# Normalisation on GpSimd, context copy on VectorE, one logits matmul per four heads, value product in four column groups, eight weight stage slots

## The reference

```python
def attention_layer(x, Wq, Wk, Wv, Wf, bf, mask):        # layers 0 and 2, 6 heads of 64
    q, k, v = heads(x @ Wq + bq), heads(x @ Wk + bk), heads(x @ Wv + bv)
    scores = einsum('bhqd,bhkd->bhqk', q, k) / sqrt(64)
    probs = softmax(scores + where(mask, 0.0, NEG))
    return merge(einsum('bhqk,bhkd->bhqd', probs, v)) @ Wf + bf

def graph_layer(x, adj, W, b, w_src, w_dst, H_w, H_b):   # layers 1 and 3, 12 heads of 32
    h = einsum('bnd,ade->bane', x, W)
    src, dst = tanh(h) @ w_src, tanh(h) @ w_dst
    a = leaky_relu(src + swap(dst), 0.2)
    a = softmax(where(adj, a, -999.0))
    f = elu(merge(a @ h) + b)
    g = sigmoid(x @ H_w.T + H_b)
    return g * f + (1 - g) * x
```

## Time and profile before

| | |
|---|---|
| median of 3 runs | 2199.91 us |
| profiled execution | 2200.55 us |
| its span, first to last instruction | 2198.6 us |
| busy: TensorE matmul / weight load | 2068.9 us (94%) / 1909.4 us (87%) |
| busy: ScalarE | 2061.2 us (94%) |
| busy: VectorE / GpSimd | 1626.4 us (74%) / 1501.2 us (68%) |
| mean granted TensorE clock | 0.98 |
| chain that ended last | PE 76%, ACT 15%, DVE 4%, POOL 2% |

### The profile page before, as it was taken

How to read it: one execution, slowest core, us unless ns; L and a number is a source line. 1 busy time by engine, 2 the same in 40 slices (tenths; PEclk the granted TensorE clock), 3 DMA queues, 4 the chain that set the end, 5 groups by cost and what they waited for, 6 DMA issues and landing times.

```text
span 2198.6 us, 57665 instructions
## 1 busy us (share of the span) xinstructions
PE 2068.9 (94%) x19852; PEld 1909.4 (87%) x19852; DVE 1626.4 (74%) x3887; ACT 2061.2 (94%) x7066; POOL 1501.2 (68%) x2698
## 2 busy tenths in 40 slices
PE   1699999999999999999769999999999999999994
PEld 1599999999999999999669999999999999999983
DVE  2377878777787878787657787878787877878774
ACT  1499999999999999999869999999999999999996
POOL 0167777777777777777546777777777777777764
PEclk9799999999999999999979999999999999999998
DMA  3100000010100000010110100000010100000000
GB/s 107 48 21 28 27 26 30 24 32 24 32 23 28 28 28 28 25 42 23 45 49 23 32 24 28 28 28 28 24 31 25 32 24 29 27 28 24 13 16 18
DMA packets 65464, 66.04 MB, mean 30 GB/s; under 512 B 22038, under 2 KB 64924, under 8 KB 65180
## 3 DMA queue, kind: packets, MB, share of 16 engines
q1 hardware_dynamic: 65180, 62.37, 9.3%
HBM read 37.18 MB, written 25.17 MB: 28 GB/s over the span
## 4 chain that ended last, share of the span: by engine, by line
PE 76%; ACT 15%; DVE 4%; POOL 2%; issue 1%; DMA 1%; SPq 1%; POOLq 0%; DVEq 0%; ACTq 0%
PE psum L642 31%; PE psum L652 15%; PE psum L634 6%; ACT LG L401 4%; PE psum L719 4%; PE psum L747 4%; PE psum L758 4%; PE psum L683 3%; ACT LA L395 2%; PE psum L694 2%; PE psum L689 2%; PE psum L703 2%; PE psum L733 1%; ACT LG L454 1%; ACT QKT L409 1%
## 5 line engine op out<-in xcount | busy, mean ns | idle before, releaser
L401 ACT ACTIVATE LG<-LG,neg_max 128x128 f32<-128x128 f32 x1536 | 601.5, 406 | 8.9 <-DVE neg_max L573 8.5
L548 DVE CUSTOM_DVE_ANT_0 LA<-psum,neg_bias 128x128 f32<-128x128 f32 x768 | 172.4, 287 | 341.6 <-PE psum L719 341.6
L376 POOL TENSOR_TENSOR prod<-th,vec 128x384 f32<-128x384 f32 x256 | 255.2, 1019 | 184.8 <-ACT th L460 184.8
L401 ACT ACTIVATION_READ_ACCUMULATOR LG<-LG,neg_max 128x1 f32 x1536 | 314.7, 205 | 0.0
L395 ACT ACTIVATE LA<-LA,neg_max 128x128 f32<-128x128 f32 x768 | 302.6, 437 | 2.4 <-DVE neg_max L548 2.4
L569 DVE COPY_PREDICATED_SCALAR LG<-no_edge,no_edge_score 128x1536 f32 x128 | 244.2, 1908 | 2.3 <-ACT LG L454 2.3
L573 DVE TENSOR_REDUCE neg_max<-LG 128x12 f32<-128x1536 f32 x128 | 224.4, 1753 | 13.6 <-DVE LG L569 0.5
L314 POOL TENSOR_SCALAR var_eps<-mv 128x1 f32<-128x1 f32 x256 | 56.8, 222 | 257.2 <-DVE mv L530 176.4
L652 PE MATMUL psum<-hT_hi,qk_hi 128*128 128x256 f32 x1152 | 208.2, 289 | 3.2 <-DVE hT_lo L516 3.2
L642 PE MATMUL psum<-hg_hi,gT_hi 128*128 128x384 f32 x768 | 203.6, 373 | 0.5 <-DVE gT_lo L553 0.5
L652 PE MATMUL psum<-hT_lo,qk_hi 128*128 128x256 f32 x1152 | 197.7, 281 | 0.0
(11 more groups left out here) (125 smaller groups left out, 6400.5 us busy)
## 6 DMA issues: line engine op xcount, KB each, us to landing
xin<-x SPq DMA_DIRECT2D x64, 192.0 KB, 2.3
x_mid<-x SPq DMA_DIRECT2D x64, 192.0 KB, 1.9
xin<-x_mid SPq DMA_DIRECT2D x64, 192.0 KB, 2.3
out<-x SPq DMA_DIRECT2D x64, 192.0 KB, 1.9
stage<-w_qk SPq DMA_DIRECT2D x8, 288.0 KB, 3.0
stage<-w_vf SPq DMA_DIRECT2D x8, 288.0 KB, 3.0
stage<-w_hg SPq DMA_DIRECT2D x8, 288.0 KB, 2.9
adj<-adj SPq DMA_DIRECT2D x32, 64.0 KB, 2.4
```

The source lines that it names most:

```text
L376: last = pool.tensor_tensor(prod[:, i, :], th[:], vec[:, r.pair(k - 2), 2 + i, :], ALU.mult)
L401: last = act.activation(head, head, ACT.Exp, bias=neg_max[:, 1, a:a + 1], accum_out=den[:, a:a + 1])
L548: last = dve.tensor_tensor_reduce(LA[:, i * N:(i + 1) * N], bank(6 + i // KC)[:, (i % KC) * N:(i % KC + 1) * N], neg_bias[:, (k) % 2, :], ...
```

## The change

- The normalisation of the attention layer's input moves from ScalarE to GpSimd, as one operation with two per-node scalars and without the ReLU; the ReLU is taken by ScalarE's copy of the transposed features and by VectorE's subtraction.
- The graph context is copied out of PSUM by VectorE.
- Logits: two transposes give source and target scores with ones beside them; VectorE multiplies the target rows by a selector into `sdR` (96 rows, 4 x 128 columns), and one matmul of 512 columns per four heads makes the whole sum.
- The value product c takes each head in two halves of 32 columns, so it uses four column groups, and stands directly behind the graph context's product.
- Stage slots: 8 instead of 2. The first pair's weights come in 14 pieces, split in steps -4 to 0. The second pair's weights are split by GpSimd in 14 steps of the first pair, kept in DRAM, and loaded in place after the last use of the old ones.
- Selectors come from the identity matrix instead of by DMA; the gate's bias is split on GpSimd, in two steps of the start.
- The order of each engine's step is new, the steps run from -5 to 133, and s runs two steps further ahead of the graph layer's stages.

```diff
+STAGES = 8
...
-        stage = sb("stage", [128, 2, KC, D // 2])
+        stage = sb("stage", [128, STAGES, KC, D // 2])
+        ahead_hi = sb("ahead_hi", [128, 2, KC, D // 2], F32R)
...
-        sel_stage = x1[0:QUADS * GROUP, 0:2, 0:4]
+        sel_stage = gate[0:ROWS, 0, 0:4]
...
-        CHANGES = {-2: range(0, 4), 0: range(4, 6), 2: range(6, 12)}
+        SPLIT_STEPS = {-4: range(0, 3), -3: range(3, 6), -2: range(6, 8), -1: range(8, 11), 0: range(11, 14)}
...
-        sdT_ps = psum[0:QUADS * GROUP, 3, 512 - N // 2:512].bitcast(BF16)
+        sdT_ps = psum[0:ROWS, 6, 512 - N:512].bitcast(BF16).rearrange("p (i n) -> p i n", i=2)
...
+            def load_piece(m):
+
+                name, region, at, n = PIECES[m % len(PIECES)]
+                if m >= len(PIECES) + STAGES:
+                    j = m - len(PIECES) - STAGES
+                    sp.wait_ge(s[f"ahead_out{j % 2}"], 32 * (j // 2 + 1))
+                elif m >= STAGES:
+                    sp.wait_ge(s["w_split"], m - STAGES + 1)
+                sp.dma_start(stage[:, m % STAGES, :, 0:n], REGIONS[region][0][m // len(PIECES)][:, at:at + n].rearrange("(c p) n -> p c n", p=128)
+                             ).then_inc(w_in[m % STAGES], 16)
+
+            def keep_piece(j):
+
+                name, region, at, n = PIECES[j]
+                sp.wait_ge(s["ahead_lo"], j + 1)
+                sp.dma_start(ahead[region, 0][:, :, at:at + n], ahead_hi[:, j % 2, :, 0:n].bitcast(F32)).then_inc(s[f"ahead_out{j % 2}"], 16)
+                sp.dma_start(ahead[region, 1][:, :, at:at + n], stage[:, (len(PIECES) + j) % STAGES, :, 0:n]).then_inc(s[f"ahead_out{j % 2}"], 16)
+
+            def load_next(name):
+
+                region, at = whole(name)
+                for i in range(2):
+                    sp.wait_ge(s[f"ahead_out{i}"], 16 * len(PIECES))
+                for i in range(2):
+                    sp.dma_start(REGIONS[region][1 + i][:, :, at].bitcast(F32), ahead[region, i][:, :, at]).then_inc(w_next[name], 16)
...
-            sp.wait_ge(s["setup_pool"], 1)
-            for i, src in enumerate((sel_src, sel_dst)):
-                rows = src.rearrange("(p k q a) n -> q (p k) a n", p=PARTS, k=2, q=QUADS)
-                for q in range(QUADS):
-                    for pk in range(2 * PARTS):
-                        at = q * GROUP + 4 * pk
-                        sp.dma_start(sel_stage[at:at + 4, i, :], rows[q, pk][:, 4 * q:4 * q + 4]).then_inc(s["const_in"], 16)
...
+                for p in range(2):
+                    if k == B - 3 + p + -1:
+                        for i in [0, 2, 1]:
+                            sp.wait_ge(s[f"qk_ps{i}"], B - 1 + p)
+                            load_next(f"c{p}{i}")
...
+                if k == B - 4:
+                    sp.wait_ge(s["m_v"], B)
+                    load_next("V")
+                if k == B + 1:
+                    sp.wait_ge(s["g_h_ps"], B)
+                    load_next("h")
+                if k == B - 1:
+                    sp.wait_ge(s["o_ps"], B)
+                    load_next("O")
+                if k == B + 1:
+                    sp.wait_ge(s["g_gate_ps"], B)
+                    load_next("gate")
...
+                    wait_latest(pool, r, ("m_hT", k + 3))
+                    b = (k + 4) % SLOTS
+                    pool.tensor_scalar(hM[:], xin[:, b, :], rstd[:, 0, b:b + 1], shift[:, 0, b:b + 1], ALU.mult, ALU.add).then_inc(s["m_h"], 1)
...
+            def head_bias(pair):
+
+                row = hb_row[:, pair, :]
+                at = 9 * pair
...
+                j, odd = divmod(k - AHEAD_STEP, SPREAD)
+                if odd == 1 and 1 <= j < len(PIECES) + 1:
+
+                    j -= 1
+                    m = len(PIECES) + j
+                    n = PIECES[j][3]
+                    src = stage[:, m % STAGES, :, 0:n]
+                    pool.wait_ge(w_in[m % STAGES], 16 * (m // STAGES + 1))
+                    if j >= 2:
+                        pool.wait_ge(s[f"ahead_out{j % 2}"], 32 * (j // 2))
+                    pool.tensor_copy(ahead_hi[:, j % 2, :, 0:n], src).then_inc(s["ahead_hi"], 1)
+                    pool.wait_ge(s["ahead_hi"], j + 1)
+                    pool.tensor_tensor(src.bitcast(F32R), src, ahead_hi[:, j % 2, :, 0:n].bitcast(F32), ALU.subtract).then_inc(s["ahead_lo"], 1)
+
...
-                    act.activation(gcT[:], bank(7)[:, 0:D], ACT.Copy).then_inc(s["gc"], 1)
-                    normed(0, k + 4, xin[:, (k + 4) % SLOTS, :], hM[:]).then_inc(s["m_h"], 1)
+                    act.activation(hT_hi[:, :, (k + 4) % 4, :], chunks(bank(2)), ACT.Relu).then_inc(s["m_hi"], 1)
...
+                    dve.wait_ge(s["g_sdT"], r.done(k - 4))
+                    dve.tensor_tensor(sdR[:, (k - 4) % 2, :, :], sdT_ps[:, 1, :].unsqueeze(1).broadcast_to([ROWS, 4, N]),
+                                      sel[:].unsqueeze(2).broadcast_to([ROWS, 4, N]), ALU.mult).then_inc(s["g_sdR"], 1)
...
+                    dve.scalar_tensor_tensor(hT_lo[:, :, (k + 3) % 4, :], chunks(bank(2)), 0.0, hT_hi[:, :, (k + 3) % 4, :].bitcast(F32),
+                                             ALU.max, ALU.subtract).then_inc(s["m_lo"], 1)
...
+                    dve.wait_ge(s["gc_ps"], r.done(k - 5))
+                    dve.tensor_copy(gcT[:], bank(7)[:, 0:D]).then_inc(s["gc"], 1)
...
+                    picks = idf[0:ROWS, 0:ROWS].rearrange("p (m a) -> p a m", a=4)
+                    dve.tensor_reduce(sel_stage, picks, AX.X, ALU.add).then_inc(s["sel"], 1)
+                    dve.wait_ge(s["sel"], 1)
+                    dve.tensor_copy(sel[:], sel_stage).then_inc(s["setup_dve"], 1)
...
-                    for q in range(QUADS):
-                        pe.matmul(bank(3 + q).rearrange("p (a n) -> p a n", a=4), sdT[rows[q], (k - 3) % 2, :],
-                                  sel_s[rows[q], :].unsqueeze(2).broadcast_to([GROUP, 4, N]), start=True, stop=False)
-                    for a in range(4):
-                        for q in range(QUADS):
-                            last = pe.matmul(bank(3 + q)[:, a * N:(a + 1) * N], sel_d[rows[q], a:a + 1].broadcast_to([GROUP, 128]),
-                                             sdT[rows[q], (k - 3) % 2, :], start=False, stop=(a == 3))
-                    last.then_inc(s["z_ps"], 1)
...
+                    for q in range(QUADS):
+                        rows = slice(q * GROUP, (q + 1) * GROUP)
+                        last = pe.matmul(bank(4 + q), sdT[rows, (k - 3) % 2, :], sdR[rows, (k - 3) % 2, :, :].rearrange("p a n -> p (a n)"), start=True, stop=True)
...
-                        half = slice(h % 2 * MD, (h % 2 + 1) * MD)
-                        last = pe.matmul(bank(2)[half, h // 2 * N:(h // 2 + 1) * N], v[:, (k - 1) % 4, h * MD:(h + 1) * MD],
-                                         PTA[:, i * N:(i + 1) * N], start=True, stop=True)
...
+                        for e in range(2):
+                            rows = slice(h % 2 * MD + e * GD, h % 2 * MD + (e + 1) * GD)
+                            last = pe.matmul(bank(0)[rows, h // 2 * N:(h // 2 + 1) * N], v[:, (k + 1) % 4, h * MD + e * GD:h * MD + (e + 1) * GD],
+                                             PTA[:, i * N:(i + 1) * N], start=True, stop=True)
...
+                    for i in range(2):
+                        last = pe.transpose(sdT_ps[:, i, :], sd3[:, (k - 2) % 4, i * ROWS:(i + 1) * ROWS], idb[:])
...
+            def weights(name, g):
+
+                if g == 0:
+                    pe.wait_ge(s["w_split"], READY[name])
+                    pe.nop(nofuse=True)
+                elif g == B:
+                    pe.wait_ge(w_next[name], 32)
+                    pe.nop(nofuse=True)
```

More of the change, by code:

```diff
@@ L268, in _ @@
+            for m in range(8, len(PIECES)):
+                load_piece(m)
             for i in range(4, SLOTS):
@@ L387, in _ @@
+            run_steps(step, setup)
         @block.scalar
@@ L772, in step @@
[L772 to L782 removed]
+                    wait_latest(pe, r, ("pt", k + 1), ("m_val", k + 3), ("g_gate", k - 3))
```

688 lines of the change are left out of this document (350 added, 338 removed).

## The result

| | before | after |
|---|---|---|
| time, median of 4 runs each (us) | 2198.84 (2195.94 to 2201.46) | 2124.06 (2123.84 to 2124.53) |
| profiled execution, its span (us) | 2200.55, 2198.6 | 2124.53, 2122.7 |
| one steady step (us) | 15.92 | 15.69 |
| s of graph 0 / graph 6 starts (us) | 72.84 / 167.77 | 45.87 / 116.29 |
| from s of graph 6 to s of graph 124 (us) | 1917.2 | 1876.2 |

The ratio is 0.9661 (95% interval 0.9644 to 0.9677): 3.4% faster, 74.8 us where 113 were forecast.

The account below looks back on a forecast made before the run. TensorE's instructions were taken as the limit, ScalarE 0.1 us behind: start -60, steady steps -38.4, middle -35.6, weight splits +15 and drain +6 make -113 from 2199.9, so 2087 us, range 2048 to 2150.

Parts of the forecast that it names:

- the likeliest case: Whole kernel: TensorE's instructions set the step, total 2087 us (2050 to 2120); chance 57%.
- the second case: Steady step: the chain over GpSimd, or VectorE, sets it at 16.0 us, splits cost 12 more, total 2147; chance 22%.
- TensorE's sum, -0.37: Steady step on TensorE: its instructions fall from 15.92 to 15.55 us (15.45 to 15.70); 15.6 was taken.
- The twelve go: -0.32: Steady step on TensorE: dropping the twelve short logits matmuls saves their 0.32 us.
- -0.15: Steady step on TensorE: a layout turn before the value product and the slow first transpose behind s go, saving 0.15 us.
- +0.10: Steady step on TensorE: the new second transpose of the score parts costs 0.10 us (0.05 to 0.15).
- Splits, +15: 14 steps of the first layer pair: weight pieces split on GpSimd in its chain add 15 us (0 to 27).
- Middle, -35.6: Weights of the second layer pair: the 38.6 us lost there go, with 3 left for a late piece.
- Start, -60: Start: small DMAs and the wait for weights go, GpSimd gets the head bias; gain 60 us (25 to 80).
- Drain, +6: End: two more short steps cost 10 us, a shorter own step saves 4 (0 to +20 together).
- the fourth: Start: it brings only its 25 us, as loads and GpSimd's bias rows queue, total 2122; chance 14%.
- The fifth: Ends and step: the ends gain but the step doesn't, as layout turns eat the twelve matmuls, total 2125; chance 2%.

Follow-up runs that it names:

- Experiment 6: The kernel before without the twelve 128-column logits matmuls of the destination scores, nothing else changed: step 15.87 us, one run of 2191.5 us.
- experiments 7 to 9: The changed kernel with the context copy, the normalisation, or both back on ScalarE: one run each, 2131.1, 2112.5 and 2154.4 us.
- Experiment 5: The changed kernel with one whole-array 512-column logits matmul replacing three on row groups from the 28th step: step 15.41 to 15.47, one run of 2105.6 us.
- experiment 4: The changed kernel with the value product in two column groups of 64 in place of four of 32: step 15.84, one run of 2139.7 us.
- experiment 3: The changed kernel with GpSimd's normalisation issued twice from the 25th step on: step 16.21, one run of 2182.3 us.
- Experiment 1: The changed kernel with GpSimd's weight split moved from the step's start to just before its wait for the exponential of y: 2104.34 us.
- Experiment 2: The changed kernel with both head-bias rows back on VectorE instead of GpSimd: 2109.56 us, ratio 0.9593 to the kernel before.

## Why the prediction was right, and where its sizes were off

Faster was right, by its mechanism: TensorE's instructions set the step, with no idle rows in it, and the time of 2124 lies in the range, but outside the likeliest case's own 2050 to 2120. The gain is 75 of 113. That the range held is in part luck: its upper end was there for the second case, a step of 16.0, which did not come, and several smaller misses filled that room. By steps:

- **TensorE and ScalarE bound together, both need relief: right.** Experiment 6 shows TensorE's alone to bring 0.05 per step, experiments 7 to 9 ScalarE's to be needed. But 0.96 us was more than was asked: one of the two moves is enough for a step of 15.69 to 15.73.
- **TensorE's sum, -0.37 (taken as -0.32): -0.23.** "The twelve go: -0.32" was mis-sized. The distance of 0.32 had a turn of the array in it that only changed its place: among whole-array products the logits' group is 0.10 longer, the one ahead of it 0.10 and the one behind it 0.10, so about 0.30 comes back. Experiment 5 prices the way in and out at 0.26. "-0.15" for the neighbours was too little: the value and graph products take 1.45 together in place of 1.60, as experiment 4 confirms, and the transposes of `hG`, no longer behind s, 0.33 in place of 0.48, which makes -0.30. "+0.10" for the second score transpose was wrong: two now take 0.11 where one took 0.15, while the probabilities' transposes, now directly ahead of s, take 0.09 longer. These distances are means over the steady steps from 700 to 1000 us in both kernels; what is left is 0.04. So the step is 15.69 where 15.60 was taken: 11 us of the 38 missed.
- **The busy times: right.** From the windows row: ScalarE 15.16 per step (15.3 was forecast), VectorE 13.66 (13.5), GpSimd 11.80 (11.7).
- **GpSimd: the second cast right, the normalisation and the slack wrong.** The cast is at 0.204 in all 128 steps: at 990.62 it no longer stands beside VectorE's product of two SBUF operands, which starts at 997.10. The Trainium skill (SBUF — State Buffer, Who interferes with whom) says that a VectorE instruction with two SBUF inputs contends with a GpSimd instruction that reads SBUF. The trace agrees. The normalisation takes 0.66, not 0.55. The chain's slack was 0.14 (experiment 3), not 0.65: the prediction closed its chain over the exponential of y, but the wait of GpSimd that ends last is that for the tanh, 0.30 us in the steady step, and so the chain runs through TensorE's products from the `hM` transposes to the graph projection.
- **Splits, +15: mis-sized, 24.5.** It follows from the slack: the pieces were a little shorter than the 27.4 said (0.67 and 1.41 us eight times, 0.51 and 1.00 six times, 25.7 together), and less 14 x 0.14 that is 23.7. The prediction's upper bound of 27 held. Experiment 1 shows the place to be the cause.
- **Middle, -35.6: right, -38.6.** The allowance of 3 for a late piece wasn't needed.
- **Start, -60: -51.5.** First transposes at 7.01 (before 12 was said). "Two bias rows of some 6 us each" was the mis-sized term: they take some 10 us each (15.5 to 25.2, 27.2 to 37.3), and start late, behind 3.98 us of waiting for their DMA. Experiment 2 shows them to be the cause: without them on GpSimd s of graph 6 starts at 103.8, earlier than the 107.5 forecast.
- **Drain, +6: +16.6**, the largest relative miss, and one on which no experiment was made. The last seven graph products start at 2037, 2054, 2070, 2082, 2092, 2103 and 2112; TensorE waits 1.4 to 3.0 us before each but one of them for ScalarE's copy L552. What was called a short step of 5 us lasts 9 to 12. That the chain through VectorE's and ScalarE's graph softmax sets them is read from the trace, not tested. TensorE's granted clock is also below full in most of these stretches (0.79, 0.79, 0.99, 0.90 and 0.63 in the five of 16 us from 2035 on; in the kernel before 0.89, 1.00 and 0.85 in the three from 2130 on), and what that adds was not separated.

Of the rivals, the second (a chain over GpSimd) came true in 14 steps only, not in the steady step; the fourth (the start brings 25) fell, although its 2122 is near the measured time: that is chance, as the time came about by four terms, the start, the step, the splits and the drain, each off by 8 to 11 us. The fifth was partly true: turns ate 0.30 of the 0.32, but others went, and the step did fall.

## What to carry to other kernels

A group of tiled matmuls has no price of its own: its distance in a timeline holds the turn of the array at its start or end, so before taking a group out, ask what will stand on either side of the rest. Where two engines are both at 100%, a change to one shows next to nothing (0.05 of 0.32 here), and once the other is relieved the first few tenths do the whole work. The slack of a chain is found by following, at each engine, the wait that ends last: here the chain went through TensorE itself, which no sum over GpSimd and ScalarE shows. Work that fits an engine's idle share must still be put into the place where the engine is idle: the same weight pieces cost 24.5 us ahead of a result that is waited for, and 4.2 in a gap of the same step.

## What the runs showed of the hardware

- Operations on three partitions are not short on GpSimd: 0.49 us for a cast, 0.90 to 0.98 for a two-input operation and 1.25 for one with a scalar column, for 384 columns. VectorE does the cast in 0.35 and a product-and-sum in 0.61.
- GpSimd's 384-column operation with two scalar columns takes 0.66, that with constants (L390) 0.51.
- Twelve products of 32 columns in four column groups (24 matmuls in the trace) did not take longer than six of 64 columns in two (12): 0.77 against 0.81 for the value product, each with what the next layout adds.
- Turns of TensorE's layout have different prices by place: 0.15 between column groups of 32 and 64, net of six matmuls fewer, and 0.26 into row groups of 32 and back to the whole array, with two matmuls fewer.
